# Quantised weights made in the gather stage and turned by DMA, in a two-layer Flamingo block on one core

## The reference, cut to what matters

```python
def _quant_act_int8(x):
    amax = jnp.maximum(jnp.quantile(jnp.abs(x), 1.0 - BOUNDARY_RANGE), EPS)
    s = QMAX / amax
    q = jnp.clip(jnp.round(x * s), QMIN, QMAX) / s
...
def _quant_w_ternary(w):
    gamma = jnp.mean(jnp.abs(w)) + EPS
    q = jnp.clip(jnp.round(w / gamma), -1.0, 1.0) * gamma
...
def _qlinear(x, w):
    return jnp.einsum('btd,hd->bth', _quant_act_int8(x), _quant_w_ternary(w))
```

## Time and profile before

| | us |
|---|---|
| Three runs: median (lowest to highest) | 1473.65 (1471.71 to 1474.03) |
| The profiled execution | 1465.63 |
| Its span, first to last instruction | 1463.8 |
| TensorE busy, VectorE, ScalarE, GpSimd | 1196.7, 952.1, 702.7, 454.7 |
| Landing of GpSimd's f loads of 512 KB, median | 5.0 |
| Landing of SP's stores of 1 MB of activations, medians | 10.0 and 8.2 |
| Mean granted TensorE clock, share of full speed | 0.904 |

### The profile page before, as it was taken

One profiled execution on the slowest core, in us unless ns is written; L12 is line 12 of the kernel. 1 busy time (PEld: TensorE's weight loads), 2 busy tenths in 40 slices (PEclk: granted clock), 3 DMA queues, 4 the chain that ended last, 5 costly groups with the idle time before them and its releaser, 6 DMA issues. The chain is left out here.

```text
span 1463.8 us, 25413 instructions
## 1 busy us (share of the span) xinstructions
PE 1196.7 (82%) x9166; PEld 887.8 (61%) x9166; DVE 952.1 (65%) x2244; ACT 702.7 (48%) x1139; POOL 454.7 (31%) x416
## 2 busy tenths in 40 slices
PE   6899999999999963899999399998141897425996
PEld 5788888888888852666664156555041686422443
DVE  5566777667677653344444279998486997366873
ACT  3233333434333321166444256766393784337991
POOL 1233333333333321011100136776200405702451
PEclk9999999999999986899999699999555899666998
DMA  5122222222222116869767899993300898744993
GB/s 207 44 87 103 74 73 73 79 94 89 98 72 73 52 58 215 312 224 323 276 232 288 322 376 317 335 331 115 135 1 1 187 367 262 211 187 154 418 356 108
DMA packets 117400, 268.17 MB, mean 183 GB/s; under 512 B 35729, under 2 KB 47153, under 8 KB 110641
## 3 DMA queue, kind: packets, MB, share of 16 engines
q1 hardware_dynamic: 103760, 228.98, 43.4%
q0 software_dynamic: 10560, 36.71, 8.0%
q10 hardware_dynamic: 2976, 1.14, 0.3%
HBM read 155.39 MB, written 105.12 MB: 178 GB/s over the span
## 5 line engine op out<-in xcount | busy, mean ns | idle before, releaser
L1847 PE MATMUL p_z<-qT,w1T 128*128 128x256 bf16 (+1 forms) x1152 | 116.2, 265 | 42.7 <-ACT third L2027 27.5
L1847 PEld LDWEIGHTS p_z<-qT,w1T 128*128 128x128 bf16 x1152 | 103.3, 99 | 55.5 <-issue 29.6
L923 PEld LDWEIGHTS p_sel<-p_pick,p_xp 128*128 128x128 bf16 x1536 | 89.3, 100 | 59.0 <-issue 34.2
L923 PE MATMUL p_sel<-p_pick,p_xp 128*128 128x128 bf16 x1536 | 100.6, 223 | 25.3 <-DVE p_pick L1045 12.5
L1061 DVE COPY p_selT<-p_sel 128x512 f32<-128x512 f32 x64 | 44.3, 692 | 104.2 <-PE p_sel L923 104.2
L2324 PE MATMUL p_o<-w2T,p_Gq 128*128 128x512 bf16 x384 | 85.7, 384 | 6.4 <-DVE p_Gq L2377 6.4
L1006 ACT ACTIVATE p_selT<-p_sel 128x512 f32<-128x512 f32 x64 | 38.2, 597 | 91.1 <-PE p_sel L923 91.1
L343 PE MATMUL p_M<-p_ctxTh,p_Wkh 128*128 128x256 f32 x256 | 75.8, 296 | 1.9 <-DVE p_Wkl L669 1.9
L343 PE MATMUL p_M<-p_xnTh,p_Wqh 128*128 128x256 f32 x256 | 75.0, 293 | 1.1 <-DVE p_V L742 1.1
L343 PE MATMUL p_M<-p_ctxTl,p_Wkh 128*128 128x256 f32 x256 | 72.9, 285 | 0.0
L343 PE MATMUL p_M<-p_ctxTh,p_Wkl 128*128 128x256 f32 x256 | 72.9, 285 | 0.0
(11 more groups left out here) (335 smaller groups left out, 3450.7 us busy)
## 6 DMA issues: line engine op xcount, KB each, us to landing
inter_d<-p_stage SPq DMA_DIRECT2D x64, 512.0 KB, 4.3
p_rows<-inter_d SPq DMA_DIRECT2D x32, 1024.0 KB, 10.8
activations<-hid SPq DMA_DIRECT2D x20, 1024.0 KB, 10.0
p_cin<-in_ctx_dram SPq DMA_DIRECT2D x32, 512.0 KB, 5.4
xparts<-p_parts SPq DMA_DIRECT2D x16, 768.0 KB, 3.2
activations<-third SPq DMA_DIRECT2D x12, 1024.0 KB, 8.2
hid<-activations SPq DMA_DIRECT2D x12, 1024.0 KB, 14.9
p_xp<-xparts SPq DMA_DIRECT2D x3, 3072.0 KB, 25.2
```

Source lines behind the costliest of these rows:

```text
L923: mm = pe.matmul(bsel[u % 2][:, k * P:(k + 1) * P], xp[:, c, tile, r, :], pick[sb % 2][:, tile, :, :].rearrange("p s g -> p (s g)"), start ...
L1847: mm = pe.matmul(bank, w1T[:, c, fc * P:(fc + 1) * P], qT[:, bass.ds(first, tiles), c, :], start=(c == 0), stop=(c == C - 1))
```

## The change

Weights are handled elsewhere.

1. **Stage one** loads w1 and w2 over SP's queue, 2 x 16 pieces of 128 x 512 (256 KB), and ScalarE sums their magnitudes, two pieces a step. Places: after the high parts of `xnT`, and at the step's end.
2. **Gather stage.** At its start TensorE sums `asum` over the partitions and ScalarE makes gamma and both thresholds. GpSimd loads the weights again (16 pieces of 512 KB), makes each piece ternary and stores it as bfloat16 (256 KB) in DRAM, one piece a step from step 2 on, the last two behind the loop. ScalarE's magnitudes leave this stage.
3. **First search.** Signs, half identity, turns and copies leave. SP issues two turning DMAs, from DRAM into `w1T` and `w2T` (2 MB each), and waits for both before the border.
4. **First product.** GpSimd's block and w2's turns leave. The estimates are summed by a matmul with ones, ahead of group 21, and read by ScalarE after group 20.
5. **End.** The skipped search and the second ffn become one branch inside ffn's block, its body in loops (`Redo`, only the test is executed here). The two borders behind ffn's go.

The core of the diff:

```diff
@@ phase1
+            def magnitude_in(b, w):
+                sp.dma_start(wabs[w][:, :], wv[w][b]).then_inc(s[f"abs_in{w}"], 16)
...
             def pre(b, par):
                 load(b, par)
+                magnitude_in(b, 0)
...
                     sp.dma_start(vrep[:, :], vg_d[b].rearrange("(a g) d -> a g d", a=1).broadcast_to([H, G, D])).then_inc(s["vrep_in"], 16)
+                    if (used := n.reuse(s["abs_done1"])) is not None:
+                        sp.wait_ge(s["abs_done1"], used)
+                        n.apart()
+                    magnitude_in(b, 1)
+                    if L:
+                        sp.wait_ge(s["abs_done0"], n.next(s["abs_done0"]))
+                        n.apart()
+                        magnitude_in(b + 1, 0)
...
+            def magnitude(b, w):
+                act.wait_ge(s[f"abs_in{w}"], n.next(s[f"abs_in{w}"], 16))
+                act.activation(wabs[w][:, :], wabs[w][:, :], ACT.Abs, accum_out=asum[w][:, bass.ds(b, 1)]).then_inc(s[f"abs_done{w}"], 1)
@@ phase2a, GpSimd
-                for m in magnitudes_in(q + 1):
-                    if m >= 2:
-                        pool.wait_ge(s["abs_done"], WN * (m - 1))
-                    pool.dma_start(wabs[m % 2][:, :, :], wv[m // WL][m % WL]).then_inc(s[f"abs_in{m % 2}"], 16)
+            def ternary(m):
+
+                w, k = m // WL, m % 2
+                pool.wait_ge(s[f"w_in{k}"], 16 * (m // 2 + 1))
+                if m:
+                    pool.wait_ge(s["tern_out"], 16 * m)
+                pool.tensor_scalar(tern[:, :, :], wabs[k][:, :, :], nth[:, w:w + 1], None, ALU.is_lt)
+                pool.tensor_scalar(wabs[k][:, :, :], wabs[k][:, :, :], th[:, w:w + 1], None, ALU.is_gt).then_inc(s["w_step"], 1)
+                pool.wait_ge(s["w_step"], 2 * m + 1)
+                pool.tensor_tensor(tern[:, :, :], wabs[k][:, :, :], tern[:, :, :], ALU.subtract).then_inc(s["w_step"], 1)
+                pool.wait_ge(s["w_step"], 2 * m + 2)
+                pool.dma_start(tv[w][m % WL], tern[:, :, :]).then_inc(s["tern_out"], 16)
+                if m + 2 < 2 * WL:
+                    load_w(m + 2)
@@ phase2a, TensorE
+            for w in range(2):
+                mm = pe.matmul(blay[0][:, w * B:(w + 1) * B], ones, asum[w][:, :], start=True, stop=True)
+            mm.then_inc(s["sums_full"], 1)
             gather(0)
@@ quantile1, SP
-            sp.dma_start(W[:, :].rearrange("p (c k) -> p c k", c=FC), w1.rearrange("(c p) k -> p c k", p=P)).then_inc(sw["w_in"], 16)
             slow.load(sp)
+            sp.dma_start_transpose(w1T[:, :, :], tern_d[0]).then_inc(sw["w_in"], 16)
+            sp.dma_start_transpose(w2T[:, :, :], tern_d[1]).then_inc(sw["w_in"], 16)
+            sp.wait_ge(sw["w_in"], 32)
@@ quantile1, ScalarE, TensorE, DVE
-                if r in SIGN:
-                    sign(SIGN[r])
...
-                    ternary_turn(pe, bturn[g % 2], signs[k % 2], halfid, g % GQ).then_inc(sw["turn_full"], 1)
...
-                    dve.tensor_scalar(w1T[:, :, g * P:(g + 1) * P], bturn[g % 2][:, :].rearrange("p (c k) -> p c k", c=C), MAGIC, MAGIC, ALU.add, ALU.subtract).then_inc(sw["turn_taken"], 1)
@@ product_tops
-MEAN_GROUP = EST_GROUPS[-1] + 4
+MEAN_GROUP = EST_GROUPS[-1] + 2
...
-                if n in W2_AFTER:
-                    turn_w2(W2_AFTER.index(n))
-                if n == EST_GROUPS[-1] + 1:
-                    sp.wait_ge(s["est_done"], 1)
-                    sp.dma_start(est_d.rearrange("(p a) -> p a", a=1), minus_t[:, :]).then_inc(s["est_out"], 16)
-                    sp.wait_ge(s["est_out"], 16)
-                    sp.dma_start(allest[:, :], est_d.rearrange("(a p) -> a p", a=1).broadcast_to([P, P])).then_inc(s["est_in"], 16)
...
+                if i == MEAN_GROUP:
+                    pe.wait_ge(s["est_done"], 1)
+                    pe.matmul(bz[i % 2][:, 0:1], ones[:, :], minus_t[:, :], start=True, stop=True).then_inc(s["est_summed"], 1)
+                for f in list(range(2, nf)) + [0, 1]:
+                    if i == MEAN_GROUP and f == 0:
+                        pe.wait_ge(s["est_read"], 1)
@@ ffn, every engine at its end
+        def again(eng, body):
+
+            eng.wait_ge(s["flag_done"], 1)
+            with eng.If(eng.value_load(flag[0:1, 0:1], min_val=0, max_val=1) > 0):
+                body(eng)
@@ feed_forward
-    quantile2_of_all(nc, flag, room, qT, w1T, K, zs, amax2)
-    ffn(nc, "p9_", Gs, spare, perm, g_d, w2T, gam, amax2, gf, x3_d, out_d, flag=flag)
```

More of the change, by code:

```diff
@@ L804, with phase2a @@
 BANK = 4
[L807 removed]
+def phase2a(nc, xparts, perm, gmask, f1, bias, f2, K, inter_d, w1, w2, asum, gam, th, nth, tern_d):
     RING, WN = 4, 2
@@ L2238, in __getitem__, with ffn @@
         return self.w[p, c, bass.ds(self.first, P)]
-def ffn(nc, prefix, Gs, spare, perm, g_d, w2T, gam, amax, gf, x3_d, out_d, flag=None, check=None):
-    cut, small, rank, flag_out = check or (None,) * 4
+def ffn(nc, Gs, spare, perm, g_d, w2T, gam, amax, gf, x3_d, out_d, cut, small, flag, rows, qT, w1T, zs, K):
+    rank, prefix = quantile_ranks(N2)[0], "p8_"
     R, QR, LAG, YR, BEHIND = len(Gs), 4, 4, 8, 2
@@ L2331, in _ @@
+            pe.wait_ge(s["asked"], 1)
+            pe.wait_ge(s["y_done"], WB * NB)
+            pe.matmul(bo[0][:, 0:1], ones[:, :], total[:, :], start=True, stop=True).then_inc(s["told"], 1)
+            again(pe, redo.on_tensor)
         @block.scalar
         def _(act):
-            with when(act, flag):
-                act.wait_ge(s["scales"], 1)
-                for n in range(NB * WB):
-                    arrived(act, n)
-                    if check:
-                        if n:
-                            act.wait_ge(s["counted"], n)
-                        act.activation(junk, tile(n), ACT.Sign, bias=below[:, :], accum_out=cnt[:, n:n + 1]).then_inc(s["counted"], 1)
-                    if by_act(n):
-                        act.activation(tile(n), tile(n), ACT.Identity, bias=magic[:, :], scale=s2[:, :]).then_inc(s["rounded_act"], 1)
-                    if n == 1:
-                        act.wait_ge(s["gf_in"], 16)
-                        act.activation(tg[:, :], gf_s[:, :], ACT.Tanh).then_inc(s["tanh"], 1)
+            act.wait_ge(s["scales"], 1)
@@ L2415, in feed_forward @@
-def feed_forward(nc, es, room, spare, qT, w1T, w2T, gam, amax1, gf, K, x3_d, g_d, est_d, out_d, w2, th, nth, perm):
+            n_ = Count(dve)
+            own = s["own"]
+            dve.memset(magic[:, :], MAGIC)
+            dve.memset(ones[:, :], 1.0)
+            dve.tensor_scalar(below[:, :], cut[:, :], -1.0, None, ALU.mult)
+            dve.reciprocal(inv[:, :], amax[:, 0:1]).then_inc(own, 1)
+            dve.wait_ge(own, n_.next(own))
+            dve.tensor_scalar(s2[:, :], inv[:, :], QMAX, None, ALU.mult).then_inc(s["scales"], 1)
@@ L2417, in feed_forward @@
+            dve.wait_ge(own, n_.next(own))
+            dve.tensor_tensor(flag[:, :], worse[:, :], small[:, :], ALU.max).then_inc(s["flag_done"], 1)
+            again(dve, redo.on_vector)
+def feed_forward(nc, es, room, spare, qT, w1T, w2T, gam, amax1, gf, K, x3_d, g_d, out_d, perm):
     sbt = lambda n, s, d=F32: es.enter_context(nc.sbuf_tensor(n, s, d))
```

528 lines of the change are left out of this document (241 added, 287 removed).

## The result

The changed kernel takes 1411.69 us (median of 4 executions, 1410.47 to 1412.67), the kernel before 1473.38 (1471.71 to 1474.03, 4 executions): ratio 0.958, 95% interval 0.957 to 0.960. The forecast was 1423, the range 1411 to 1443: faster, as foretold, but only 0.7 us above the lower end. Over all comparisons of this study, which measured both kernels again, the changed kernel took 1412.3 (14 executions) and the kernel before 1470.6 to 1472.3.

The account below looks back on a forecast made before the run. Bounds by stage: TensorE in stage one, VectorE with TensorE and ScalarE in the search, a queue-order hole in the product. Terms 0.5 + 2.8 - 11.9 - 36.5 - 5.7 = -50.8 from 1473.65 gave 1423 us, range 1411 to 1443.

Parts of the forecast that it names:

- The hole: First product: ScalarE's 28.36 us wait for the estimates, laid to SP's queue order; 29.6 us go, 0.4 allowed for the matmul.
- The product's tail and front: First product: next stage at 1268 against 1302.48 (-34.5), front -2 without w2 loads; together -36.5, bounds -29 and -41.
- The first search: First search: 16 rounds shrink from 72.9 us to 61.0 at 3.81 each, without signs and turns: -11.9.
- The turns: First search: two DMA turns take 30 us, hidden under 70, cost 0; outlasting it: slower 0.05, partial loss 0.08.
- the estimate of 437 us: First search: both turns' time on the issuing engine if the skill's tile were a 256-byte packet; the forecast doubted this reading.
- Stage one: Stage one: ScalarE's 32 magnitudes fit its idle time, SP's 32 loads cost a little: +0.5, bounds 0 and 26.
- The gather: Gather: start +2.8 from two loads of w; GpSimd keeps pace at 9.4 of 13.62 us: 0, bound +8.
- the rival: Gather: GpSimd's passes 1.6 times as long beside VectorE's work, 14.1 us a step, +10 to +20; chance 0.06.
- The end: After the flag: 10.8 us shrink to one test and border, 5.15 us: -5.7, bounds -3.5 and -8.
- From the profile to the median: Whole kernel: the median, 1473.65, lies 8.0 above the profiled 1465.63; the -50.8 is carried over unchanged, giving 1423.

Follow-up runs that it names:

- the variant: The changed kernel with GpSimd's first two loads of w leaving only after the second block of activations has landed: 1410.6 us (10 executions) against 1412.3 (14).
- the silent end: The changed kernel without loading or comparing GpSimd's last four pieces of w2, so its DMAs stop from about step 14 of the gather: 1412.23 us (5 executions).
- the first experiment: The kernel before, unchanged, run again with a profile of its own: median 1472.29 us (10 executions), its profiled execution 1475.19.

## Why the forecast was right or wrong

**The hole: right in place, chain and size.** From the first product to the end of the last Gelu 146.9 us became 116.8, 30.1 less, against 29.2 foretold (29.6 less 0.4). But its cause was told too simply. "The order of the queue costs the time" does not stand: the order alone made the kernel slower (15.5 us of wait left, the turns later), and without any round trip for the estimates the next stage still began at 1300.1, 2.4 us earlier. Two bounds lay one upon the other: the estimates, and behind them GpSimd's signs, the turns and 6 MB of stores. The change takes away both at once, and so the sum came out; the forecast had looked at only one of them.

**The product's tail and front: mis-sized by 3.** I let the last store land up to 10 us after 1259 and the next stage begin 8.8 us behind the last Gelu. It begins 5.7 behind it (1250.81 to 1256.47): without turns the stores land in 7.1 us (the last four in 5.6), and VectorE's border is a bare one of 1.28. The front gave 2.0 as foretold (8.3 to 6.3 us from the border to the first product). Term: -40.5 measured, -36.5 foretold, bound -41.

**The first search: right.** -11.8 against -11.9, rounds of 3.82; this is read from the rounds, and no run takes the signs and turns away alone. **The turns: hidden, as foretold**, in 18 us, not 30. The Trainium skill (DMA: Bandwidth & Descriptors, the section on the increment by 16) charges a turn within SBUF of 8,192 tiles 262,144 cycles on the issuing engine. A turn here, from DRAM, put 8,320 packets on the queue and held SP 7.75 us, so the estimate of 437 us is refuted; the turns within SBUF, which the sentence is about, had said so in the qT rows (1.23 us at the least for 256 KB), so a tile there is not such a packet. The forecast misread one row: the 8448 packets for 2.10 MB belong to eight turns of 256 KB, not nine, of which the ninth was only issued in that window. That changes nothing in the sum.

**Stage one: right within its scatter.** Its last transpose begins at 558.1 in the shown profile, and between 557.4 and 561.0 in seven others of the changed kernel and its variants, against 558.0 to 558.8 before: -1 to 3, with a median near 1, foretold 0.5. TensorE is not short of anything; ScalarE's idle time behind both magnitudes shows it.

**The gather: start right, end too optimistic.** +2.5 for the start (foretold 2.8, shown by the variant). For the end I took 0 because the last store of the weights would have landed by 811; it has (issued at 804.31, and such a store lands within 4.9 us), and no one waits for it. What I left out is that it and its loads share the DMA engines with the stores of `inter_d`, which set the pace there: +2.4 at full clock (of which the silent end, one profile, takes back 1.5), within the bound of +8. GpSimd never paces a step: 9.4 us of 13.62, and 3.32 idle; in the first steps, which are only 10.0 us apart, it falls behind with its loads of f (604.83, 615.23, 626.69, 637.57), and no step comes later for it. The contention that the Trainium skill names (GPSIMD Engine Reference, Specifications) does show, but on the other engine than the rival had it: VectorE's picks, 1.22 us each in the kernel before, take 2.93 and 2.50 where they begin during GpSimd's pass with two inputs (L926), which itself keeps its 2.13. In the run with the silent end such a pass begins 0.16 us into a pick and takes 3.04, and the pick 1.22. So of two instructions with two inputs the one that comes second waits for the other; beside GpSimd's passes with one input a pick takes 1.22 to 1.85. It costs no step: the picks stay 13.63 us apart.

**The end: mis-sized by 2.** 3.0 us are left of 10.8 where I left 5.1: the border behind the first search, from which I took that price, was not a fit measure. Bound -8, measured -7.8, and -7.7 alone.

**From the profile to the median: the largest error.** The sum by the profiled executions was near, -50.8 against -53.2. But I wrote of the median that it "lies 8.0 above, and I carry differences over unchanged". By the medians that the forecast used the gain is 62.0 (1473.65 - 1411.69), by the profiled executions 53.0 (1465.63 - 1412.67), foretold 50.8 for both. So 11.2 us are missing: 2.2 in the terms and 9.0 in this step, 8.0 of them from the kernel before and 1.0 from the changed kernel, whose profiled execution lies above its own median. Of the 8.0, 1.4 to 3.1 are a high median of three executions, since it came out at 1470.6 to 1472.3 later. The rest is the quick execution. Against the slow one of the first experiment it had 3.0 at the gather's end and 4.0 in the first product; but the profile of the end alone, an execution in the middle of its ten, has a short hole (28.61) and the slow clock, and four of six profiles of the kernel before and its variants have the full clock, so what sets the quick one apart from the middle is not shown. Nor is it shown that the hole takes its scatter away with it: without a hole, TensorE's sum alone still scatters over 7.9 us. The range held by 0.7 us, and only because its low end was made of the bounds of the product and the end; that was luck as much as care.

## What to carry to other kernels

A wait of 28 us in front of an engine says what comes last there, not what it is worth: ask what is ready next when it is gone, down to the last store in the queue, and count the bytes behind it. Here TensorE's sum alone gave 3 us and a new order of the queue alone a loss; taking the weights out of the stage gave 30.6, and together with TensorE's sum 40.5. And before carrying a difference from a profile to a median, see where that profile lies among the executions, and take a second one if it lies outside them.

## What the hardware showed that I had not expected

- A turn of 2 MB of bf16 from DRAM: SP 7.75 us, landed after 9.8 to 10.7, the DMA engines moving 290 GB/s; ten of them 90 us. A turn of 512 KB within SBUF, among stores, held SP between 1.33 and 15.75 us.
- A store of 0.5 KB took 18 us to be acknowledged behind five stores of 1 MB issued within 9 us, and 10.5 behind five issued within 14 us.
- VectorE's pick (bf16, two inputs) took 2.93 us instead of 1.22 when it began during GpSimd's pass with two inputs, and the pass 3.04 instead of 2.13 when it began during a pick.
- The kernel before scatters by 10 us over 31 executions: in its profiles and those of its variants TensorE's clock from 785 to 800 us is 1.00 in some and 0.77 in others while it does the same work with the same pauses (matmuls of 1.13 us, 0.87 to 0.89 us apart, ahead of the fall in both), and the hole is between 28.4 and 31.7 us. What decides about the clock there stays open.
